# The experts' down product as a product of high and low parts, with W_down fetched for each tile

## The reference, cut to what matters

```python
routing = jax.nn.softmax(xf @ router_w.T, axis=-1)
top_w, top_i = lax.top_k(routing, 2)            # 2 of 8 experts for each token
top_w = top_w / jnp.sum(top_w, axis=-1, keepdims=True)
g = jnp.einsum('nd,ehd->neh', xf, w_gate)       # d = 256, h = 512
u = jnp.einsum('nd,ehd->neh', xf, w_up)
h = jax.nn.silu(g) * u
y = jnp.einsum('neh,edh->ned', h, w_down)
out = jnp.einsum('ned,ne->nd', y, combine)
```

## Time and profile before

| | us |
|---|---|
| median of 3 runs | 2455.37 |
| lowest and highest | 2454.93, 2455.67 |
| the profiled execution | 2449.71 |
| its span in the trace | 2447.6 |
| stretch of the tile loop in `Experts` | 958.5 to 1331 |
| one tile in that loop | 5.19 |

### The profile page before, as it was taken

How to read it: one execution, slowest core, us unless ns; L and a number is a source line. 1 busy time by engine, 2 the same in 40 slices (tenths; PEclk the granted TensorE clock), 3 DMA queues, 4 the chain that set the end, 5 groups by cost and what they waited for, 6 DMA issues and landing times. The chain is left out here.

```text
span 2447.6 us, 102597 instructions
## 1 busy us (share of the span) xinstructions
PE 2277.6 (93%) x43872; PEld 1863.5 (76%) x43872; DVE 1744.6 (71%) x3606; ACT 1351.1 (55%) x3754; POOL 870.3 (36%) x769
## 2 busy tenths in 40 slices
PE   7999999999988975999998799999999789999997
PEld 6888888888875554888886577777777578888886
DVE  5777777778786785222223688888888678888876
ACT  5656666666644543333332677777777255555555
POOL 3333333333322221333443633444423454333330
PEclk9999999999999986999999999999999999999998
DMA  6455555555423336111113688887777421222220
GB/s 205 139 157 157 154 151 158 157 148 160 104 74 98 107 109 262 51 48 49 48 50 101 189 237 245 233 232 224 229 215 207 145 88 72 80 80 81 80 81 28
DMA packets 220595, 332.48 MB, mean 136 GB/s; under 512 B 33640, under 2 KB 112108, under 8 KB 218864
## 3 DMA queue, kind: packets, MB, share of 16 engines
q1 hardware_dynamic: 213328, 309.12, 41.5%
q0 software_dynamic: 6816, 16.79, 2.1%
HBM read 170.72 MB, written 78.77 MB: 102 GB/s over the span
## 5 line engine op out<-in xcount | busy, mean ns | idle before, releaser
L868 ACT ACTIVATE prob_x<-ps_score_x,neg_max_x 128x257 f32<-128x257 f32 x1024 | 403.5, 480 | 200.8 <-DVE neg_max_x L940 200.3
L940 DVE TENSOR_REDUCE neg_max_x<-ps_score_x 128x2 f32<-128x514 f32 x512 | 328.8, 683 | 101.4 <-PE ps_score_x L747 100.2
L758 PEld LDWEIGHTS ps_v_x<-v_wide_x,probT_x 128*32 128x32 f32 x18432 | 288.1, 108 | 127.8 <-issue 119.4
L758 PE MATMUL ps_v_x<-v_wide_x,probT_x 128*32 128x68 f32 x18432 | 335.5, 223 | 25.0 <-issue 16.7
L964 DVE STREAM_TRANSPOSE probT_x<-prob_x 128x1152 f32<-128x1152 f32 x256 | 344.1, 1344 | 0.0
L1104 POOL TENSOR_TENSOR ctxT_x_lo<-ready,ctxT_x_hi 128x514 fp32r<-128x514 f32 x128 | 153.1, 1196 | 367.9 <-ACT ctxT_x_hi L847 299.0
L1104 POOL TENSOR_TENSOR split<-loaded,split 128x514 fp32r<-128x514 f32 x128 | 153.7, 1201 | 324.8 <-ACT split L847 314.2
L2603 POOL TENSOR_TENSOR cells_s<-cells_s,moved_s 128x512 f32<-128x512 f32 x128 | 174.6, 1378 | 261.0 <-DMA moved_s<-w_s 225.9
L1220 ACT ACTIVATE loaded<-loaded,neg_max_s 128x32 f32<-128x32 f32 x512 | 156.6, 308 | 124.6 <-DVE neg_max_s L1209 124.6
L240 PE MATMUL ps_x<-split,w_q_x_hi 128*128 128x258 f32 x1024 | 208.0, 300 | 11.7 <-POOL split L1104 8.8
L2020 DVE TENSOR_TENSOR hid_moe<-ps_up_moe,silu_moe 128x512 f32<-128x512 f32 x71 | 49.1, 692 | 202.6 <-PE ps_up_moe L240 202.6
(11 more groups left out here) (309 smaller groups left out, 5754.3 us busy)
## 6 DMA issues: line engine op xcount, KB each, us to landing
v_wide_x<-v_x SPq DMA_DIRECT2D x512, 76.5 KB, 2.2
v_out_x<-v_x SPq DMA_DIRECT2D x128, 306.0 KB, 4.2
v_wide_x<-v_out_x SPq DMA_DIRECT2D x512, 76.5 KB, 3.3
ready<-ctx SPq DMA_DIRECT2D x128, 257.0 KB, 3.6
loaded<-ctx SPq DMA_DIRECT2D x128, 257.0 KB, 4.1
moved_s<-w_s SPq DMA_DIRECT2D x256, 128.0 KB, 2.1
gate_whole<-moe_experts SPq DMA_DIRECT2D x32, 256.0 KB
lo_out<-gate_whole SPq DMA_DIRECT2D x32, 256.0 KB
```

The lines of the kernel that those rows point to most:

```text
L758: ins = pe.do.matmul(self.ps_v[r * T:(r + 1) * T, b % 2, :, :], self.probT[b % 3][:, r, n * T:(n + 1) * T], self.v_wide[b % 4][:, :, r, n, ...
L868: act.do.activation(self.prob[b % 3][:, r, 0:S], self.ps[:, r, 0:S], ACT.Exp, bias=self.neg_max[b % 2][:, r:r + 1]).then_inc(*s.exp.at(tag ...
L940: dve.do.tensor_reduce(self.neg_max[b % 2][:, r], self.ps[:, r, 0:S], AX_X, ALU.max, negate=True).then_inc(*s.neg_max.at(tag, b, half))
```

## The change

W_down is no longer kept in SBUF for all experts. The host hands it over as a tensor of its own (`moe_down`, 128 rows for each expert), and in `Experts` SP fetches for every tile the 512 KB of the tile's expert into one of four buffers `w_raw`. The place comes from a register that SP loads from `w_row`, a new row of the plan. From the fifth tile on SP waits before each fetch until VectorE is through with the buffer. ScalarE makes the high part of the fetched block (`w_down_hi`) between the high part of x and `hidT`, VectorE the low part. `hidT` gets a high part (ScalarE, from PSUM) and a low part (VectorE, from PSUM and the high part). `down` becomes a split product: 12 float32r matmuls of 256 columns in place of 4 plain ones. The buffers lie where W_down of all experts lay. `down` waits for `hidT`'s high part and for `down_lo`, the new count of VectorE's low parts. VectorE's order is now: low part of `hidT`(t - 1), `hid`(t), low part of x(t + 1), `y`(t - 1), low part of W_down for t. Seven counts of the last stage become one (`bit_row`), with the same waits.

```diff
-        begin, down, end = e * W_EXPERT, e * W_EXPERT + 2 * W_GATE, (e + 1) * W_EXPERT
-        sp.do.dma_start(w[:, begin:down], self.lo_out[:, 2 * e * W_GATE:2 * (e + 1) * W_GATE]).then_inc(*self.s.e_in.at(e, "lo"))
-        sp.do.dma_start(w[:, down:end], self.experts[e][:, 2 * W_GATE:]).then_inc(*self.s.e_in.at(e, "others"))
+        begin = e * W_EXPERT
+        sp.do.dma_start(w[:, begin:begin + 2 * W_GATE], self.lo_out[:, 2 * e * W_GATE:2 * (e + 1) * W_GATE]).then_inc(*self.s.e_in.at(e))
...
     def sync(self, sp):
+        s = self.s
         self.gates.fetch_hi(sp, self.gate_hi[:, :].bitcast(F32), self.up_hi)
+        sp.wait_ge(s.plan, "w_row")
+        for t in range(N_TILES):
+            row = self.nc.values_load(self.w_row[0:1, t:t + 1], engines=[mybir.EngineType.SP], min_val=0, max_val=(E - 1) * P,
+                                      skip_runtime_bounds_check_because="it is an expert's number, at most E - 1, times its rows")
+            if t >= 4:
+                sp.wait_ge(s.down_lo, "w", t - 4)
+            sp.do.dma_start(self.w_raw[t % 4], self.w_down[bass.ds(row, P), :]).then_inc(*s.w_fetched[t % 4].at(t))
         self.load_next(sp)
...
-            pe.wait_ge(s.hidT, t)
+            pe.wait_ge(s.hidT, t, "hid")
+            pe.wait_ge(s.down_lo, "hid", t)
             if emptied:
                 pe.wait_ge(*emptied)
-            for k in range(KH):
-                ins = pe.do.matmul(bank[:, 0:D], self.hidT[t % 2][:, k, :], self.w[:, bass.ds(base + (2 * W_GATE + k * D), D)],
-                                   start=k == 0, stop=k == KH - 1)
-            ins.then_inc(*s.y_ps.at(t))
+            split_product(pe, bank[:, 0:D], lambda k: self.hidT[t % 2].pair(lambda a: a[:, k, :]),
+                          lambda k: self.w_split[t % 2].pair(lambda a: a[:, k * D:(k + 1) * D]), KH).then_inc(*s.y_ps.at(t))
...
-            act.wait_ge(s.hid_turned, t)
+            act.wait_ge(s.w_fetched[t % 4], t)
             if t >= 2:
                 act.wait_ge(s.y_ps, t - 2)
-            act.do.activation(self.hidT[t % 2][:, :, :], banks["hid", t][:, :].rearrange("p (k q) -> p k q", q=P), ACT.Copy).then_inc(
-                *s.hidT.at(t))
+            act.do.activation(self.w_split[t % 2].hi, self.w_raw[t % 4], ACT.Copy).then_inc(*s.hidT.at(t, "w"))
+            act.wait_ge(s.hid_turned, t)
+            act.do.activation(self.hidT[t % 2].hi[:, :, :], banks["hid", t][:, :].rearrange("p (k q) -> p k q", q=P), ACT.Copy).then_inc(
+                *s.hidT.at(t, "hid"))
...
+        def hidT_lo(t):
+            dve.wait_ge(s.hidT, t, "hid")
+            dve.do.tensor_tensor(self.hidT[t % 2].lo[:, :, :], banks["hid", t][:, :].rearrange("p (k q) -> p k q", q=P),
+                                 self.hidT[t % 2].hi[:, :, :].bitcast(F32), ALU.subtract).then_inc(*s.down_lo.at("hid", t))
+
+        def w_lo(t):
+            dve.wait_ge(s.hidT, t, "w")
+            dve.do.tensor_tensor(self.w_split[t % 2].lo, self.w_raw[t % 4], self.w_split[t % 2].hi.bitcast(F32), ALU.subtract).then_inc(
+                *s.down_lo.at("w", t))
+
         for t in range(N_TILES + 1):
+            if t:
+                hidT_lo(t - 1)
...
                 dve.do.tensor_copy(self.y[n % 3][:, :], banks["y", n][:, 0:D]).then_inc(*s.y.at(n))
+            if t < N_TILES:
+                if t >= 2:
+                    dve.wait_ge(s.y_ps, t - 2)
+                w_lo(t)
```

More of the change, by code:

```diff
@@ L179, in __init__ @@
         self.plan = count("plan", [*grid(("placed",), s), ("zero",), ("tiles",), *grid(("ends",), range(4)), *grid((
-            "all_places", "at_own", "slot", "tile_f", "tile", "row", "passed", "owner", "w_at", "hi_at", "over", "pair", "second",
+            "all_places", "at_own", "slot", "tile_f", "tile", "row", "passed", "owner", "w_at", "hi_at", "w_row", "over", "pair", "second",
             "from_token", "to_pair"))])
@@ L184, in __init__ @@
             count(n, grid(chunk)) for n in ("row_hot", "tile_hot", "coded_row", "coded_group", "decoded"))
-        self.e_in = count("e_in", grid(range(E), ("lo", "others")) + [("gate_hi",), ("up_hi",)], 16)
+        self.e_in = count("e_in", grid(range(E)) + [("gate_hi",), ("up_hi",)], 16)
         self.gate_in = count("gate_in", grid(range(N_SPLIT)), 16)
@@ L191, in __init__ @@
         self.x_turned, self.gate_ps, self.up_ps, self.silu, self.hid, self.hid_turned, self.hidT, self.y_ps, self.y = (
-            count(n, grid(tile)) for n in (
+            count(n, grid(tile)) if n != "hidT" else count(n, grid(tile, ("w", "hid"))) for n in (
                 "x_turned", "gate_ps", "up_ps", "silu", "hid", "hid_turned", "hidT", "y_ps", "y"))
+        self.w_fetched = [count(f"w_fetched{i}", grid(tile[i::4]), 16) for i in range(4)]
+        self.down_lo = count("down_lo", [event for t in range(N_TILES + 1) for event in [
+            *[("hid", t - 1) for _ in range(min(t, 1))], *[("w", t) for _ in range(t < N_TILES)]]])
         self.y_in, self.y_scaled, self.y_half, self.y_added, self.y_first = count("y_in", grid(s, ("x", 0, 1)), 16), count("y_scaled", grid(s[1:], range(2))), count("y_half", grid(s[1:])), count("y_added", grid(s[1:])), count("y_first", grid(range(2)))
@@ L209, in __init__ @@
         self.bit_rstd = count("bit_rstd", grid(units, ("rstd", "shift")))
-        self.bit_var, self.bit_xn, self.bit_top, self.bit_a, self.bit_inv, self.bit_back, self.bit_z0, \
-            self.bit_z1, self.bit_z = (count("bit_" + n, grid(units)) for n in (
-                "var", "xn", "top", "a", "inv", "back", "z0", "z1", "z"))
+        self.bit_var, self.bit_xn = (count("bit_" + n, grid(units)) for n in ("var", "xn"))
+        self.bit_row = count("bit_row", grid(units, ("top", "a", "inv", "back", "z0", "z1", "z")))
         self.stored = count("stored", grid(units), 16)
@@ L1764, in __init__ @@
         self.up_hi = X[:, :, :].rearrange("p g d -> p (g d)")
+        free = [w.begin + (e * W_EXPERT + 2 * W_GATE) * 4 for e in range(E)]
+        self.w_raw = [nc.alloc_sbuf_tensor_at(f"w_raw{i}_moe", [P, KH * D], F32, offset=free[i])[:, :] for i in (0, 1, 6, 7)]
+        self.w_split = [Split(nc, None, None, None, [nc.alloc_sbuf_tensor_at(
+            f"w_down{i}_{part}_moe", [P, KH * D], F32R, offset=free[2 * i + n])[:, :] for n, part in ((2, "hi"), (3, "lo"))]) for i in range(2)]
         self.ends = [sb(f"ends{i}", [P, 2 * E]) for i in range(2)]
@@ L1783, in __init__ @@
         self.hid = [sb(f"hid{i}", [P, HID]) for i in range(2)]
-        self.hidT = [sb(f"hidT{i}", [P, KH, P]) for i in range(2)]
+        self.hidT = [Split(nc, stack, f"hidT{i}_moe", [P, KH, P]) for i in range(2)]
         self.y = [sb(f"y{i}", [P, D]) for i in range(3)]
@@ L1838, in turn_hid @@
         def turn_hid(t):
-            bank, emptied = banks.take(("hid", t), s.hidT, t)
+            bank, emptied = banks.take(("hid", t), s.down_lo, "hid", t)
             pe.wait_ge(s.hid, t)
@@ L1866, in tensor @@
         turn_x(0)
-        base = None
         for t in range(N_TILES + 1):
-            before = base
             if t < N_TILES:
@@ L1877, in tensor @@
             if t:
-                down(t - 1, before)
+                down(t - 1)
             if t < N_TILES:
@@ L2688, in build @@
             with ExitStack() as own:
-                run(Experts(nc, own, s, X, consts, gates, routed, places, w, xn_out, y_out, load_next))
+                run(Experts(nc, own, s, X, consts, gates, routed, places, w, a["moe_down"], xn_out, y_out, load_next))
         with ExitStack() as late:
```

42 lines of the change are left out of this document (23 added, 19 removed).

## The result

| | before | changed |
|---|---|---|
| median of the runs beside each other | 2455.15 us (4 runs, 2449.31 to 2455.67) | 2429.73 us (4 runs, 2427.36 to 2432.94) |
| profiled execution (span) | 2449.71 us (2447.6) | 2427.36 us (2425.6) |

The ratio is 0.9892, with a 95% interval of 0.9867 to 0.9917. The kernel is faster by 1.1%, 25.4 us between the medians and 22.35 us between the profiled executions. The forecast was 20.7 us less, 2434.7 us, with a range of 2430.0 to 2446.0; the measured median lies 0.27 us under the range.

A forecast was written before the change was run, and what follows sets the result against it. TensorE was taken to bound the tile loop. Terms -20.5 (down product), -1.0 (start) and +0.75 (end) gave -20.7 us: 2449.7 to 2429.0 profiled, then 2434.7 us with the median's 5.7 added; range 2430 to 2446.

The forecast's parts named there:

- The bound: Experts' tile loop: TensorE, busy 370.33 of 372.52 us, bounds it, so shorter TensorE work shortens the loop one to one.
- TensorE's term, 69 x 0.297: Down product in the tile loop: 1.72 us becomes 1.42, tile 5.19 becomes 4.89, saving 20.5 us over 69 products.
- ScalarE and VectorE: Added high and low parts in each tile: 1.05 us on ScalarE, 1.22 and 0.69 on VectorE, all covered.
- loop of 2.84 + L: Chain per tile through down product, copy and VectorE's low parts, W_down's taking L; TensorE's 4.89 us stays longer below L 2.05.
- Rivals 1: VectorE's cover partly used up beside POOL: W_down's low part 2.2 us, tile 5.04, time 2445 us; chance 0.10.
- rival 2: VectorE held behind both POOL instructions: W_down's low part 3.27 us, tile 6.11, time 2519 us; chance 0.04.
- rival 3: Fetch of x in the loop lands late, after 6.0 us: tile 5.20, about 2456 us, no change; chance 0.05.
- Lx: Landing time of the fetch of x in the loop: covered while under 5.4 us; 2.8 median, 4.7 at most.
- The start, -1.0: Loop's start: first x could land in 2.8 us instead of 4.7, a gain between 0 and 1.9, taken as 1.0.
- The end, +0.75: Loop's end: the last tile's low parts have no next tile to hide under, so the last copy comes 0.75 us later.
- rival 4: Experts' stage opens sooner because earlier loads are shorter and first loads land early: 2 to 4 us more, 2431; chance 0.05.
- 5.7 above the profiled one: Whole kernel: the runs' median 2455.37 us exceeds the profiled execution by 5.7; carried over, it turns 2429.0 into 2434.7.

The follow-up runs named there:

- doubled low part: The changed kernel with VectorE computing the low part of W_down twice per tile, into the same place: 2455.34 us (one run), tile 5.27 us.
- one block ahead: The changed kernel with SyncE waiting for the low part of tile t - 1, not t - 4, before each W_down fetch: 2501.49 us (one run).
- two blocks ahead: The changed kernel with SyncE waiting for the low part of tile t - 2, not t - 4, before each W_down fetch: 2433.86 us (one run).

## Why the prediction was right, and where not

**The bound.** Right. TensorE bounds the loop before and after; a shorter down product shortens the tile one to one, and the plain product on the same fetches gives nothing back (0.9994).

**TensorE's term, 69 x 0.297.** The step was undersized by a tenth: 0.326 for a tile, and -22.39 us for the loop in place of -20.5. The steps of 0.118 are as in the earlier trace rows. I had counted twelve of them and left the 0.22 us between turned x and down product as it was. It became 0.13, the first step 0.21, and eleven steps 1.29: 1.63 from turned x to `turn_hid`, where 1.94 - 0.297 would have been 1.65. The other 0.02 to 0.03 lie at the joins to the gate product. What has to be compared is the distance between the neighbours of the replaced work, not the work alone; 0.05 us for a tile at the joins was in the forecast's own bounds, as a loss.

**ScalarE and VectorE.** Right: 1.05, 1.22 and 0.68 us against 1.05, 1.22 and 0.69, all covered, with 1.07 us to spare at `hid` (0.9 forecast). The doubled low part put the loop of 2.84 + L to the test within 0.05 us.

**Rivals 1 and 2, VectorE and POOL in each other's way.** They do meet, but the other way about: the low part keeps its 1.22 us and POOL's `y_out`, which starts 0.88 us after it, grows from 1.02 to 1.22. Without the low part beside it (the plain product, and the low part ahead of the copy) it is 1.02 again. The Trainium skill ("SBUF — State Buffer", section "Who interferes with whom") has VectorE with two SBUF inputs and a GpSimd instruction that reads SBUF exclude each other, the first one keeping on. The traces agree with that for a low part that began first: in all eleven profiles with the low part POOL's instruction is longer by what the low part still had to run, less 0.11 to 0.13 us, from 0.20 in the changed kernel (0.33 to run) to 1.05 with one block ahead (1.17 to run). The other way round they don't: where POOL's instruction had begun 0.02 to 1.0 us before, the low part kept 1.22 to 1.24 us, both with the doubled low part and with one block ahead; only where both began within 0.04 us of each other did it take up to 1.30. So rival 2, which holds VectorE behind both instructions, doesn't occur in any run. POOL has idle time before and behind, so nothing follows in the changed kernel.

**SP, DMA and the fetch of x (rival 3).** Right that it is covered: the blocks land in 3.6 us where 16.9 are free, and even 7 would do (two blocks ahead). Lx grew from 2.8 to 3.4 in the loop, far from 5.4. It isn't the amount of traffic that does it: with the plain product (151 GB/s) and with the low part ahead of the copy (158 GB/s) x lands in 2.8 us as before, and there the last block is sent 2.4 and 2.3 us ahead of the fetch of x; in the changed kernel it is 1.0 us ahead (3.4 us), and with the doubled low part 0.2 us behind (4.0). `y_out` shows the same: it lands in 2.5 us before the change, in 4.4 with the block sent 0.5 us after its start, and in 2.7 with the doubled low part, where the block goes 1.75 us after it although the instruction takes the same 1.22 us. So what a small transfer meets is the single block sent close to it; this is read from five profiles, and no run moved the block alone.

**The start, -1.0.** Wrong in sign, +2.48. The step of the mechanism that failed is "it could land in 2.8 us in place of 4.7, but four new blocks go out at that very time. Gain between 0 and 1.9": I had bounded a gain and excluded a loss without a reason, though the earlier trace rows had loads of 512 KB at 6.0 and 8.5 in crowded stretches. How soon the first x is used after its issue follows the blocks sent ahead of it: 3.4 to 3.8 us with none or one, 4.27 with two, 7.0 to 7.8 with four. Without the four the start is 1.1 to 1.4 shorter than before, which is the gain I had put down.

**The end, +0.75.** +0.44 in the first profile, of the size forecast, since the down product comes 0.30 earlier and the low parts took what I counted. Two other profiles have 6.8 to 6.9 in place of 5.8, by the fall of the clock in the pause ahead of the last product. That was in no term.

**The sum and the range.** By stretches: forecast -20.5, -1.0, +0.75 = -20.75; measured -22.39, +2.48, +0.44 = -19.5. Two misses cancelled, so that the sum came within 1.3 us is luck. The step that put the median outside the range is the last one, "5.7 above the profiled one; I take the difference over to it", and the range built on it. The profiled execution was forecast at 2429.0 and took 2427.36, 1.6 less, through the 2.5 us outside the three stretches, against 1.3 too little inside them; the median was to lie 5.7 above it and lies 2.4 above it, 3.3 less. The 5.7 was one profiled execution of the kernel before against three runs, no property of the kernel, and the range gave no room to scatter. The measured time is nearest to rival 4's 2431, but rival 4's mechanism is refuted: the loop opens 2.5 us later after `from_token`, not sooner. The changed kernel's three medians are 2429.73, 2434.36 and 2433.83, with single runs from 2425.69 to 2439.03, and before's runs go from 2440.27 to 2464.01. The code ahead of `from_token` is the same in the changed kernel and all its variants, and in their twelve profiles `from_token` comes anywhere between 948.14 and 953.53 us. The mean is 950.8, the 950.68 of the profile of before, so neither do the loads that went from the stage ahead of it give anything there. A range of 2430 to 2446 about a forecast of 2434.7 wanted 3 to 4 us more at its low end for that alone. So the 5.0 us between the forecast and the first median aren't explained by any mechanism of the change; what moves the time from run to run stays open. The two later medians are within 0.9 us of the forecast.

## What to carry to other kernels

Cost a replaced piece of work by the distance between its neighbours in the trace, before and after, and not by its own duration alone. When loads move out of a prologue into a loop, look at what else is on the way at the loop's first iteration: four blocks, of which the first is used 14 us after the first fetch of x goes out (964.30 against 950.24), hold up that small fetch, for which every engine waits, by 3.5 us, and one wait on the loading queue gives it back. And put the spread of repeated runs into the range as a term of its own.

## What the runs showed of the hardware that I had not expected

- An indirect fetch of 128 rows is used 7.0 to 7.8 us after its issue behind 2 MB of queued loads, and 4.27 behind 1 MB. In the loop it lands in 2.8 us at 49 and at 151 to 158 GB/s alike, as long as the last block of 512 KB went out 2.3 us or more ahead of it; with 1.0 us it is 3.4.
- After the same pause of 1.86 us TensorE's granted clock stayed at 2.4 GHz through the next product in one profile of the changed kernel (steps of 0.118 us) and fell to 1.2 in two (0.214): 1.0 us of difference with the same code. At the loop's start the granted clock rose 3.0 to 6.2 us after the first gate product.
- POOL's indirect DMA instruction (1.02 us) grows beside a VectorE subtraction of two SBUF inputs that began before it, by what the subtraction still has to run less 0.11 to 0.13 us: to 1.22 us for `y_out`, to as much as 2.07 for the fetch of x. Where POOL began first, the subtraction kept its 1.22 to 1.24 us.
- Taking that meeting away made the loop 4.7 us longer, twice: one wait of 1.7 to 1.8 us for x, and many late gate products. TensorE's register read ahead of the gate product, 0.30 us in the changed kernel, then falls beside POOL's fetch of x and takes up to 0.55. That POOL's fetch is the reason was not tested.
